# Wide attention: subtraction of the maxima on 32-row tiles, an even stream of maxima, and the additions laid between and beside them

## The reference, cut to what matters

```python
def _L3_attn_ref(x, adaptive_scale, Wq, bq, Wk, bk, Wv, bv, Wo, bo, gamma, beta):
    B, N, _ = x.shape
    Q = (x @ Wq.T + bq).reshape(B, N, H, HD)
    K = (x @ Wk.T + bk).reshape(B, N, H, HD)
    V = (x @ Wv.T + bv).reshape(B, N, H, HD)
    scores = jnp.einsum('bnhd,bmhd->bhnm', Q, K)
    scores = scores * (SCALE * adaptive_scale)[None, :, None, None] / TEMP
    w = jax.nn.softmax(scores, axis=-1)
    attn = jnp.einsum('bhnm,bmhd->bnhd', w, V).reshape(B, N, H * HD)
    y = x + (attn @ Wo.T + bo)
    ...
    return (y - mu) / jnp.sqrt(var + EPS) * gamma + beta
```

## Time and profile before

| | us |
|---|---|
| runs | 6013.05, 6019.32, 6021.36 |
| median | 6019.32 |
| profiled execution | 6014.71 |
| its span in the profile | 6012.9 |
| the changed stage, first score to last sums | about 3984 to 5461 |

### The profile page before, as it was taken

How to read it: one execution, slowest core, us unless ns; L and a number is a source line. 1 busy time by engine, 2 the same in 40 slices (tenths; PEclk the granted TensorE clock), 3 DMA queues, 4 the chain that set the end, 5 groups by cost and what they waited for, 6 DMA issues and landing times. The chain is left out here.

```text
span 6012.9 us, 88536 instructions
## 1 busy us (share of the span) xinstructions
PE 5556.6 (92%) x33238; PEld 2845.6 (47%) x33238; DVE 3960.6 (66%) x6791; ACT 2749.5 (46%) x4388; POOL 1089.8 (18%) x731
## 2 busy tenths in 40 slices
PE   6999998788989999989999899979999999997999
PEld 2343333345557777752222277733343433434676
DVE  6777775775577777779999523267777777773412
ACT  4656565222233333347777633334444444442333
POOL 0110100120022322311220000023434333341000
PEclk7999999788989999999999899989999999998999
DMA  3211110001111111101111100000000000001000
GB/s 86 45 30 29 30 29 11 0 0 22 35 38 25 28 30 25 33 17 36 35 36 30 33 1 1 1 23 12 15 8 15 12 12 12 12 15 36 4 4 8
DMA packets 119148, 131.42 MB, mean 22 GB/s; under 512 B 44580, under 2 KB 67924, under 8 KB 118404
## 3 DMA queue, kind: packets, MB, share of 16 engines
q1 hardware_dynamic: 118216, 125.07, 9.8%
q10 hardware_dynamic: 504, 0.69, 0.1%
HBM read 102.29 MB, written 22.07 MB: 21 GB/s over the span
## 5 line engine op out<-in xcount | busy, mean ns | idle before, releaser
L583 DVE TENSOR_REDUCE l_max_parts<-l_p 128x2 f32<-128x1024 f32 x512 | 602.4, 1219 | 188.6 <-PE l_p L559 152.7
L730 ACT ACTIVATE attn_w<-l_p 128x512 f32<-128x512 f32 x1024 | 554.7, 596 | 366.2 <-PE l_p L720 254.6
L3456 DVE TENSOR_REDUCE wide_max_parts<-wide_p 128x2 f32<-128x1024 f32 x512 | 613.8, 1219 | 133.2 <-PE wide_p L3360 120.8
L2403 PE MATMUL caus_p<-caus_x_one,big 128*128 128x129 f32 x4608 | 637.7, 285 | 0.0
L2488 ACT ACTIVATE big<-caus_p 128x512 f32<-128x512 f32 (+3 forms) x768 | 345.7, 489 | 600.9 <-PE caus_p L2389 448.6
L2403 PEld LDWEIGHTS caus_p<-caus_x_one,big 128*128 128x128 f32 x4608 | 588.4, 198 | 35.4 <-issue 2.1
L583 DVE TENSOR_REDUCE rot_max_parts<-rot_p 128x2 f32<-128x1024 f32 x488 | 574.0, 1218 | 46.7 <-PE rot_p L559 44.5
L2848 ACT ACTIVATE moe_hidden<-moe_experts,moe_b 128x512 f32<-128x512 f32 x512 | 351.0, 687 | 527.4 <-PE moe_experts L2836 527.3
L3379 PE MATMUL wide_p<-wide_q,wide_k 64*128 64x512 f32 x2048 | 529.2, 595 | 0.0
L3559 ACT ACTIVATE attn_w<-wide_p 128x1024 f32<-128x1024 f32 x342 | 350.1, 1024 | 354.6 <-PE wide_p L3379 351.0
L2858 PEld LDWEIGHTS moe_experts<-big,moe_hidden 128*128 128x128 f32 x4096 | 474.2, 192 | 50.3 <-issue 49.2
(11 more groups left out here) (540 smaller groups left out, 8314.9 us busy)
## 6 DMA issues: line engine op xcount, KB each, us to landing
pair_q_stack<-q_parts SPq DMA_DIRECT2D x576, 32.0 KB
pair_k_stack<-k_parts SPq DMA_DIRECT2D x576, 32.0 KB
wide_inverse<-inverse_rows SPq DMA_DIRECT2D x64, 256.0 KB
l_q_stack<-q_parts SPq DMA_DIRECT2D x279, 32.0 KB
l_k_stack<-k_parts SPq DMA_DIRECT2D x279, 32.0 KB
big<-in_L_ffn_W SPq DMA_DIRECT2D x32, 256.0 KB, 5.6
q_parts<-pair_parts_q SPq DMA_DIRECT2D x8, 768.0 KB, 3.6
k_parts<-pair_parts_k SPq DMA_DIRECT2D x8, 768.0 KB, 3.6
```

Of the source, the lines that this page charges most:

```text
L583: self.nc.vector.tensor_reduce(self.max_parts[:, 2 * p:2 * p + 2, n, half], pair[:, :, 0:self.width(n, half)], AX.X, ALU.max).then_inc(*se ...
L730: self.nc.scalar.activation(self.exps[t % len(self.exps)], bank, ACT.Exp).then_inc(*self.exped.up())
L2403: mm = nc.tensor.matmul(outs[o % 2][:, nq % 2 * (C + 1):(nq % 2 + 1) * (C + 1)], exps[h % 2][:, kb, nq * P:(nq + 1) * P], x_one[b % 2][:, ...
L3456: nc.vector.tensor_reduce(max_parts[:, :, n, h], side, AX.X, ALU.max).then_inc(*maxed.up())
```

## The change

The subtraction of the maxima is done once for both halves of a key block. The rows of maxima are split in four quarters of 32 partitions (two heads by two halves), 512 columns each, and at half 0 four matmuls with 32 rows each write into the slots of both scores. PE therefore waits for both slots before the first of them. The send takes eight transfers instead of four. The bf16 copies of q and k and the buffer `max_parts` become double, so that maxima can run across the border of a unit. Four maxima of unit 1 are issued before unit 0, and from there on each key block has two: one before weigh and one after it. The send moves from block 7 to block 6. The three projections move to blocks 3, 4 and 5, between the scores and the first maximum, and so do sums (block 1) and the steps of `later` (blocks 0, 2 and 7). DVE's addition for a block moves to the next block, after its scores and ahead of its first maximum; POOL's addition goes beside that maximum.

```diff
-    q_bf, k_bf = st.sbuf("q_bf", [P, T], BF16), st.sbuf("k_bf", [P, T], BF16)
+    q_bf, k_bf = ([st.sbuf(f"{n}_bf{i}", [P, T], BF16) for i in range(2)] for n in "qk")
-    max_rows = [st.sbuf(f"max_rows{i}", [P, T], BF16) for i in range(2)]
+    max_rows = [st.sbuf(f"max_rows{i}", [P, BANK], BF16) for i in range(2)]
+    quarter = [slice(j * P // 4, (j + 1) * P // 4) for j in range(4)]
-    MAXIMA = [3, 2, 3, 2, 2, 2, 2, 0]
...
+    stream = [("max", u, t) for u in range(1, len(units)) for t in range(TILES)]
+    def maxima(n):
+        out = []
+        for _ in range(min(n, len(stream))):
+            out.append(stream.pop(0))
+            out += beside(out[-1])
+        return out
-    plan = project(0) + [("max", 0, t) for t in range(TILES)] + [("send", 0)] + project(1)
+    plan = project(0) + [("max", 0, t) for t in range(TILES)] + [("send", 0)] + project(1) + maxima(4)
+    added = []
     for u in range(len(units)):
-        todo = list(range(TILES)) if u + 1 < len(units) else []
         for kb in range(NT):
-            for h in range(HALF):
-                plan.append(("score", u, kb, h))
-                for _ in range((MAXIMA[kb] + h) // HALF if todo else 0):
-                    plan.append(("max", u + 1, todo.pop(0)))
-                    plan += beside(plan[-1])
-            plan += beside(None)
-            if kb == NT - 1 and u + 1 < len(units):
-                plan.append(("send", u + 1))
-            if u + 2 < len(units):
-                if kb == NT - 1:
-                    plan += [("project_k", u + 2), ("project_v", u + 2)]
+            plan += [("score", u, kb, h) for h in range(HALF)]
+            if kb == 1:
+                plan += [("sums", u - 1)] if u else []
+            elif kb in (3, 4, 5):
+                plan += [project(u + 2)[kb - 3]] if u + 2 < len(units) else []
+            elif kb != NT - 2:
+                plan += next_later()
+            plan += added + maxima(1) + beside(None)
+            if kb == NT - 2:
+                plan += [("send", u + 1)] if u + 1 < len(units) else []
             if kb:
-                plan += [("weigh", u, kb - 1), ("add", u, kb)]
-                waiting.append((u, kb))
-                if kb == NT - 2 and u + 2 < len(units):
-                    plan.append(("project_q", u + 2))
+                plan.append(("weigh", u, kb - 1))
+                added, pooled = [("add", u, kb)], [(u, kb)]
...
+            plan += maxima(1) + gate_work(IN_TILE)
-            if u and kb == 1:
-                plan.append(("sums", u - 1))
-            elif u and kb == 3:
+            if u and kb == 2:
                 plan.append(("invert", u - 1))
-            elif u and kb == 5:
+            elif u and kb == NT - 2:
                 plan.append(("divide", u - 1))
...
-                    for a in range(2):
+                    n = NT // HALF
+                    for j in range(4):
                         for r, part in enumerate((max_hi, max_lo)):
-                            row = a * WIDE + r
+                            row = j * P // 4 + r
...
-                    for a in range(2):
-                        nc.tensor.matmul(side[:, a, :], ones_bf[own[a], :], max_rows[u % 2][own[a], cols],
-                                         start=True, stop=False)
+                    if h == 0:
+                        _, i_next, left_next = plan[n_step + 1]
+                        if left_next and new(*left_next):
+                            pe.wait_ge(*left_next[0].at(left_next[1]))
+                        for half, to in enumerate((side, slots[i_next])):
+                            for a in range(2):
+                                rows_of = quarter[HALF * a + half]
+                                nc.tensor.matmul(to[:, a, :], ones_bf[rows_of, :],
+                                                 max_rows[u % 2][rows_of, :], start=True, stop=False)
```

More of the change, by code:

```diff
@@ L3149, in wide_attention @@
     att = st.sbuf("att", [P, PAIRS, T])
-    max_parts, neg_max = st.sbuf("max_parts", [P, 2, NT, HALF]), st.sbuf("neg_max", [P, 2 * NT])
+    max_parts = [st.sbuf(f"max_parts{i}", [P, 2, NT, HALF]) for i in range(2)]
+    neg_max = st.sbuf("neg_max", [P, 2 * NT])
     max_hi, max_lo = (st.sbuf(n, [2 * NT, P], BF16) for n in ("max_hi", "max_lo"))
@@ L3228, in wide_attention @@
                     finish(units[u - 1][0])
-            else:
-                plan += next_later()
+            waiting += pooled
     while work or later:
@@ L3233, in wide_attention @@
     last = len(units) - 1
-    plan += beside(None)
+    plan += added + beside(None)
     plan += [("weigh", last, NT - 1), ("keep", last), ("sums", last), ("invert", last), ("divide", last)]
@@ L3333, in _ @@
             pe.wait_ge(*ones_set.at(1))
-            for (kind, *args), i, left in plan:
+            for n_step, ((kind, *args), i, left) in enumerate(plan):
                 side = None if i is None else slots[i]
@@ L3359, in _ @@
                     for a in range(2):
-                        mm = nc.tensor.matmul(side[:, a, :], q_bf[own[a], n * P:(n + 1) * P],
-                                              k_bf[own[a], h * BANK:(h + 1) * BANK], start=True,
+                        mm = nc.tensor.matmul(side[:, a, :], q_bf[u % 2][own[a], n * P:(n + 1) * P],
+                                              k_bf[u % 2][own[a], h * BANK:(h + 1) * BANK], start=True,
                                               stop=True)
@@ L3370, in _ @@
                     u, kb, h = args
-                    for sem, n in ((q_kept, u + 1), (k_kept, u + 1), (row_sent, 64 * (u + 1))):
+                    for sem, n in ((q_kept, u + 1), (k_kept, u + 1), (row_sent, 128 * (u + 1))):
                         if new(sem, n):
@@ L3436, in _ @@
                     v.wait_ge(*q_kept.at(u + 1))
-                    if u:
-                        v.wait_ge(*max_scored.at(TILES * u))
-                    nc.vector.tensor_copy(q_bf[:, :], q[u % SLOTS][:, :]).then_inc(*q_cast.up())
+                    if u > 1:
+                        v.wait_ge(*max_scored.at(TILES * (u - 1)))
+                    nc.vector.tensor_copy(q_bf[u % 2][:, :], q[u % SLOTS][:, :]).then_inc(*q_cast.up())
                 elif kind == "project_v":
@@ L3453, in _ @@
                     v.wait_ge(*max_scored.at(TILES * u + t + 1))
-                    if u and new(joined, u):
-                        v.wait_ge(*joined.at(u))
-                    nc.vector.tensor_reduce(max_parts[:, :, n, h], side, AX.X,
+                    if u > 1 and new(joined, u - 1):
+                        v.wait_ge(*joined.at(u - 1))
+                    nc.vector.tensor_reduce(max_parts[u % 2][:, :, n, h], side, AX.X,
                                             ALU.max).then_inc(*maxed.up())
@@ L3466, in _ @@
                     if u:
-                        v.wait_ge(*row_sent.at(64 * u))
+                        v.wait_ge(*row_sent.at(128 * u))
                     nc.vector.tensor_copy(max_hi[:, :], side[0:2 * NT, 0, 0:P]).then_inc(*hi_kept.up())
@@ L3548, in _ @@
                                          bias=bk[:, m:m + 1]).then_inc(*k_kept.up())
-                    if u:
-                        a_.wait_ge(*max_scored.at(TILES * u))
-                    nc.scalar.activation(two(k_bf[:, :]), side, ACT.Identity,
+                    if u > 1:
+                        a_.wait_ge(*max_scored.at(TILES * (u - 1)))
+                    nc.scalar.activation(two(k_bf[u % 2][:, :]), side, ACT.Identity,
                                          bias=bk[:, m:m + 1]).then_inc(*k_cast.up())
```

10 lines of the change are left out of this document (5 added, 5 removed).

## The result

The changed kernel takes 6481.8 us (median of four runs, 6469.4 to 6487.0) against 6020.3 for the kernel before (6013.1 to 6024.3): a ratio of 1.077, 95% interval 1.075 to 1.078. The forecast was 6368 us, range 6200 to 6440. It is slower, as forecast, and by the mechanism forecast, but by 461 us and not by 348, and outside the range. The profiled execution has a span of 6485.3 us instead of 6012.9, so the traces differ by 472 us. The changed stage holds all of it: it ran from 3984 to 5461 us and now runs from 3984 to 5932, that is 1948 us instead of 1477.

What follows compares the result with a forecast made beforehand. PE was taken to bound the kernel nearly everywhere. Work 0.5, waits 8.05 and clock 1.9 gave 10.45 us in 30 units, 314; with 25, 5 and 4 together 348, so 6368 us, range 6200 to 6440.

Steps and rivals of the forecast that it cites:

- The walk of the slots: Following the three ring slots through a unit's blocks: PE waits 3.15, 2.5, 1.6 and 0.8, together 8.05 us a unit.
- PE's work: Matmul work per unit: the saved subtraction pair is spent on tile-shape changes, moved projections and sums add 0.44; 0.5 more.
- Rival (c): PE's work alone sets the time, 64- and 32-row tiles mixing without a gap: 39 us less, 5980; chance 0.06.
- (d): Tile-shape changes cost nothing but waits stay, five of eight blocks saving 0.21: about 40 us less, 6325; chance 0.05.
- the clock's term: Two waits a unit over 2.29 us, each bringing a clock fall in 7/9 of cases at 1.23: 1.9 us a unit.
- Rival (a): The same waits between dense stretches, but the clock stays full: 291 us more, 6310; chance 0.15.
- The bound of 2.29: PE idle times from 2.29 us usually brought a clock fall in the stage before; those of 1.25 to 2.10 never did.
- a blocked step costs up to 2.3 ... I take 25: At three batch ends, 11 DVE steps of `later` each stand ahead of the add, inside POOL's time: 25 us in all.
- Twice two gate steps at send, 0.4 in 14 units: 5: At the send, DVE's small router steps delay 14 units by 0.4 us each: 5 us in all.
- rival (e): Worse: the send's wait brings falls too, or shape changes and four subtractions cost more: up to 6440 us; chance 0.09.
- (b): POOL is not in the way of DVE: waits 1.85, 1.1, 1.6, 0.8, no clock falls: 6230 us; chance 0.13.
- (f): The change does nothing to the whole kernel, gains and waits cancel: 6019 us; chance 0.02.

Runs made afterwards that it cites:

- e1: Changed kernel with the three projections of blocks 3, 4 and 5 behind the first maximum: 6211.3 us, ratio 1.033 to the kernel before.
- e2: Changed kernel with POOL's additions of blocks 3 and 5 released by the second maximum, not the first: 6326.6 us, ratio 1.052 to the kernel before.
- e5: e1 with the send ahead of block 6's first maximum: 6182.4 us, ratio 1.027 to the kernel before.
- e12: e10 with the change's four 32-row subtractions side by side and eight transfers: 6111.3 us, ratio 1.016 to the kernel before.
- e10: e5 with the divide in block 4, 64-row subtraction pairs, send behind weigh, batch-end steps last in their blocks: 6022.1 us, ratio 1.001 to the kernel before.
- e4: Changed kernel with 12 spare pairs of matmuls filling PE's waits in blocks 4 and 6: 6363.6 us, ratio 1.058 to the kernel before.
- e3: Changed kernel with the old 64-row subtraction pairs, each score waiting for its own slot, four transfers: 6312.7 us, ratio 1.049 to the kernel before.
- e6: e1 with the divide at the end of block 4 instead of 6: 6175.0 us, ratio 1.025 to the kernel before.
- e13: e10 with gate steps spread unevenly, none in blocks 4 to 6: 6012.5 us, ratio 0.9991 to the kernel before.
- e14: e13 with one batch-end step moved from block 5 to block 1: 6013.7 us, ratio 0.9989 to the kernel before.

## Why the prediction was right in direction and too small in size

**The waits held.** The walk of the slots gave 3.15, 2.5 and 1.6 for blocks 3, 5 and the send; the trace has 3.22, 2.62 and 1.50, and e1, e2 and e5 take each of them away or change it by the amount that its cause has in the walk. The fourth, 0.8 ahead of a unit for eight transfers, is 0.17. This is the case that was left open: shorter rows are issued faster, 0.61 apart (4105.02 to 4105.63 in the changed kernel's SP queue) and not 0.72, and what is left is the divide's 0.2. Together 7.51 against 8.05. How much of the eight transfers' cost is left without the other waits is another matter: e12 has 1.43 there.

**PE's work was a little more.** A plain block takes 4.65, not 4.56. Its parts: the four subtractions take 4120.99 - 4120.67 = 0.32, which is 0.21 as for a pair and 0.11 for the change from 32-row to 64-row tiles, and 4125.32 - 4124.99 = 0.33 from the maximum to them holds the other 0.11. (Of the 0.32 only the sum is measured; the split takes the gap behind to be the one ahead.) So the sum of both values taken from the earlier trace rows was right: the pair saved is spent on the two changes. The Trainium skill (TensorEngine Tiling, Tiling Modes) has a change of mode drain the engine; the trace agrees, with 0.11 on each side of the four subtractions. What was not foreseen is 0.09 to 0.11 between the two scores: one behind the other they take 4122.81 - 4120.99 = 1.82, and with a pair ahead of each 1.71 (e10). Rival (c), the mixture without a gap, and (d), changes at no cost, fall with this. Whether the second score's weights load later when no bf16 pair stands ahead of it was not tested. Work is 8 x 0.08 (4.65 less 4.57) + 0.44 = 1.08 a unit, against 0.5 forecast: 17 us in all.

**The step that failed is the clock's term**, "Two of my waits are over 2.29: 2 x 7/9 x 1.23 = 1.9 a unit". In the quiet units it measures 4.45 (e4), and by the runs the clock gives back 118 us where 57 were forecast. Three things in it were too small. *How often.* Over the whole stage the chance was about right: counted where the matmuls right behind a wait take longer than usual (a pair of scores over 2.1 us instead of 1.99), waits near 2.62 were followed by a fall in 28 of 41 cases, those near 3.22 in 32 of 39. But in the quiet units it was 16 of 16, which makes 2 x 1.23 = 2.5. *What a fall costs.* 1.23 is what one projection lost in a fall that began before PE was back (at 4479.59), so that a part of it cost nothing. The windows of the kernel before on both sides of the one in the earlier trace rows show it:

```profile
4478.00:4480.00 2.00, 0.41 (x2) 0.75 0.00 0
...
4482.00:4484.00 2.00, 2.00 (x13) 0.90 0.02 2
```

At 0.75 the clock stood at 0.50 for 1 of the first 2 us, of which PE was working for 0.41. e2 has 1.65 for one fall, and the quiet unit of 55.62 us with two falls of some 3 us is 3.4 above e4's 52.24, 1.7 each. *How long it lasts.* Five of the sixteen falls lasted some 7 or 10 us, which is the last 1.1 a unit.

What makes these five long stays open. The forecast counted the third wait, 1.5 at the send, as harmless, and in the fall shown above it comes while the clock is at 0.50. But that fall began about 4152.5 (0.63 in the window from 4152) and the third wait at 4157.78, so it had already lasted over 5 us, longer than the short ones last in all; and the three of 7 us have no idle time in them behind the first wait. Whether the third wait prolonged the two longest is not shown. Rival (a), that the clock stays, falls with the counts above.

The bound of 2.29 below which nothing falls was no bound either. e2's waits of 1.87 were followed by a fall in 14 of 31, e3's of 2.06 in 23 of 56, and e1's of 1.50 in none of 30, by the same count.

**Two terms were left small: "a blocked step costs up to 2.3 ... I take 25" at the batch ends, and "Twice two gate steps at send, 0.4 in 14 units: 5".** The second counted the steps as a delay that adds up. But two of them, 0.28 us, turn round the order in which DVE and POOL come to SBUF, and that became 2.45 (e6). The lock itself was in the forecast; the Trainium skill (SBUF — State Buffer, Who interferes with whom) says that the engine that issues first keeps the ports, and the trace agrees to 0.23 us on one side and 0.05 on the other. What was missing is to ask at each place by how much the winner wins. In the sum, though, the four units with gate steps alone lie only 5 us above four quiet ones, because they lose less to the clock: it stands at 0.93 in their mean, against 0.91 in the quiet ones. The larger part lies around the batch ends: 65 us above the quiet units in eighteen units, ten of them with gate steps as well, in place of 25. How these 65 divide between the two kinds of step was not separated.

The difference, then, of the trace's 472 to the 348. All waits of PE in the stage sum to 329 us instead of 37, so they are 293 of the 472; the forecast had 276 (242, 25, 5 and 4). Work is 32 (30 x 1.08) instead of 15. What is left is the clock, 147 instead of 57. The granted clock of the trace says nearly the same: between the first and the last transpose it stands at 0.50 for 336 us, 31 of them idle, against 31 and 6 before, and half of the difference in busy time is 140. Of the 124 us missing in the forecast, 90 are clock, 17 work and 17 waits. The range ended at the 6440 of rival (e), which made the clock or the changes of shape dearer, but the clock not by as much.

**The other rivals.** (b) was the right account of the waits without POOL, and e2 shows them (1.87 and 1.17), but POOL was in the way. (c) asked whether PE's work alone sets the time. e10 shows an order with the even stream of maxima and no wait in the quiet units: 43.55 a unit, and with what e13 and e14 add at best 0.1% under the kernel before. (f) had nothing for it.

## What to carry to other kernels

When two steps trade places in a shared list, walk the order of every engine, not of the one that the trade is for: what decided here was two small DVE operations that came to stand ahead of a reduce on which PE's next slot hung. Where two engines share a port, note by how much the one that should win wins; a margin of 0.2 us was turned round here by two small steps, and losing it costs the whole of the other's operation. And price a fall of the clock over all the work that it covers, and not by one matmul in it: 1.23 was read from one projection, and a whole short fall cost 1.65 to 1.7. Here filling the waits with spare matmuls gave 118 us back.

## What the runs showed of the hardware

- Four 32-row matmuls of 512 columns side by side, with 64-row tiles ahead of and behind them, take 0.43 us with the gaps on both sides, which is two pairs of 64-row ones. With the same gap of 0.11 behind as ahead, the four alone take the 0.21 of one pair. The gain was spent exactly.
- After idle times of PE of 1.87 and 2.06 us the clock fell in a bit under half the cases, and after 1.50 never in 30, though the work around was the same. One fall of some 3 us cost 1.65 us (e2). Most falls lasted that long, but five of the sixteen in the quiet units of the changed kernel some 7 or 10.
- Row transfers issued from SP follow each other at 0.61 us when a row has half the length, and at 0.72 at the full length; so twice as many take 1.7 times the time.
- A tiny operation with two inputs on SBUF is held up beside POOL as long as a wide one: in e13 one of DVE's norm operations on 128x8 elements, 0.17 otherwise, takes 2.24 and ends 0.02 after POOL's addition:

```profile
4482.38 0.17 DVE L201 SCALAR_TENSOR_TENSOR wide_square<-wide_square,wide_std 128x8 f32<-128x8 f32 x1
4482.58 2.24 DVE L204 SCALAR_TENSOR_TENSOR wide_rstd<-wide_square,wide_rstd 128x8 f32<-128x8 f32 x1
4482.45 2.35 POOL L3281 TENSOR_TENSOR big<-big,attn_w 128x1024 f32<-128x1024 f32 x1 [3.60 <-PE wide_p L3366]
```
